# A third order table for a four-layer attention and mixture kernel: new marks for the same 5036 steps, all row fills in one run, and explicit waits where buffers are reused

## The chip, the cores and the metric

One Trainium2 chip, one core. The metric is the device time of one launch in microseconds, the median of the runs. A profile of one more execution gives the span from the first to the last instruction.

## The reference, cut to what matters

Eight batches of 256 tokens with 256 features pass four layers. Each layer is an attention with 16 heads of 16 features against a context of the same size, followed by a feed-forward part, and the feed-forward parts differ.

```
layer 0: x += attention(layernorm(x), ctx), causal;  x += layernorm(x) @ sign(W)
layer 1: x += attention(...), causal;                x += two shared experts + the best 2 of 16 experts
layer 2: x += attention(...), masked, q/k/v normed;  x += quantised gated product, 1024 wide, ternary weights
layer 3: x += attention without projections;         x += three blocks, each norm, gelu, two 256x256 products
```

The 16 experts of layer 1 are sparse: each token's row is copied to a place that depends on its expert, the rows are worked in 31 tiles of 128 rows for each half of the batches, and the results are copied back and added with their weights.

## The kernel before, in words

The kernel keeps the whole of `x` in SBUF. Its work is cut into 5036 **steps**, and a step is one method of a `Part` class. Every engine has its own `Part` with its own methods, so that a step is one engine's piece of work: `score` and `maxima` are TensorE's, `exp` and `projected` ScalarE's, `reduce` and `normalise` VectorE's, `k_low`, `scatter` and `fetch` GpSimd's, and `k_stack`, `fill`, `tile_load` and the other transfers SyncE's.

The steps stand in 378 **lanes**. A lane is a generator that gives its steps in a fixed order (the lane `exponents` gives all 512 `exp` steps, the lane `tile` those of one tile). The tuple `AT` holds for each lane one number, here called a **mark**, for each of its steps. `program` sorts all marks of all lanes and calls the steps in that order. Each engine's instruction stream is thus what is left of the sorted list when only its own steps are kept, and an engine never takes a step before the one ahead of it. The marks come from a planner that isn't part of the file. On the chip they mean nothing but order, with one exception: `claim` chooses the PSUM bank of a new tile by comparing marks with `DRAIN`, 0.6 after the mark of the step that empties a bank.

What must not happen before something else is said by semaphores. Where a buffer is reused and the code has no wait, the order of the table together with other waits keeps the two apart.

The order of attention is `ORDER`: 32 items (layer, batch), layers 0 and 1 mixed in the first half and 2 and 3 in the second. For each item:

- `k_hi`/`q_hi` (ScalarE, line 1931 to 1948), `k_rest`/`q_rest` (VectorE), `k_low`/`q_low` (GpSimd, 2658 and 2660) split keys and queries in three bf16 parts.
- `k_stack` and `q_stack` (SyncE, 2890) copy the parts to the stacked operands, six transfers of 128 KB each.
- 16 x `maxima` (TensorE, 1580) and `reduce` (VectorE, 2247, 2255 or 2259) find row maxima, and `turn_max` (1669) and `rows` (ScalarE, 2027) turn them.
- 16 x `score` (1598 with 1601 or 1604) and `exp` (ScalarE, 2010) follow, and then `values` (1688), `copy_output`, `output`, `normalise`, and the projection `project_in`, `projected`, `project_out`, `project_add`.

Beside attention run the fills (12 transfers from `wo` that give the two row buffers in HBM defined contents, line 2942), the raw weights of layer 2 (`raw_load`, 2983), 32 `scatter` and 32 `fetch` steps (GpSimd's indirect transfers, 2803 and 2816), and the tiles: `gather` loads an expert's weights (384 KB), `tile_load` a tile's rows (2960), `tile_turn`, `tile_up` and `tile_down` are its products, and `tile_store` writes it back. At the very end the last batch's three blocks run in two halves of 128 tokens (`half_in`, `half_turn`, `half_out` and so on, lines 1869 and 1874), and between exponentials and gelus ScalarE loads another function table.

`wait_score` on GpSimd, ahead of every `scatter` and `fetch`, waits for the last `score` whose mark lies before that of the step.

Of the kernel before, what the change touches and what calls it, by code (L numbers as in the profile page):

```python
# [12 lines left out]
P = 128  # L13
# [85 lines left out]
class Signal:  # L99
# [8 lines left out]

    def at(self, key):

        return self.sem, self.unit * (self.known.get(key, 0) + 1)
# [3 lines left out]
AT = (  # L115
# [1096 lines left out]
def build(nc, known, x_d, ctx_t_d, ctx_d, mask_d, mask_t_d, w_d, wo_d, vec_d, col_d, gate_d,  # L1212
          expert_d, wq_gate_d, wq_up_d, wq_down_d, w3_d, scale3_d, la_d, lb_d, out_d):
    made = {}
    with ExitStack() as ctx:
# [206 lines left out]
        def tile_of(key):  # L1422
            return ps[:, bank_of[key], :]
# [1695 lines left out]
```

## Time and profile before

| what | value |
|---|---|
| runs | 1161.19, 1162.01 and 1164.85 us; median 1162.01 |
| profiled execution | span 1166.1 us, 26103 instructions; no other time is given for it |
| busy | TensorE 1050.5, VectorE 903.8, ScalarE 804.5, GpSimd 564.1 us |
| TensorE's granted clock | 0.970 of full over the span |
| DMA | 140.03 MB, mean 120 GB/s |

The span is the time of one execution with the profiler on. A busy time is that of an engine's instructions; matmuls overlap, so that the busy time of TensorE is longer than the least time between its issues.

### The profile page before, as it was taken

The numbers are of one execution on the slowest core, as the hardware profiler recorded it, in microseconds if no ns is written. First come the engines' busy times: TensorE is split into PE (matmuls) and PEld (weight loads), VectorE is DVE, ScalarE is ACT, GpSimd is POOL, SyncE is SP. The second block draws the span as 40 slices with busy tenths as digits, with TensorE's granted clock in tenths as the row PEclk, the third lists the DMA queues.
The fourth block names the chain that finished last, engine by engine and source line by source line (L and its number), as shares of the span: only waits on it lengthen the run. The fifth ranks groups of instructions, "written<-read, shape, count | busy, mean of one in ns | idle before, by whom it ended". The sixth has DMA issues, their size and how long they took to land.

```text
span 1166.1 us, 26103 instructions
## 1 busy us (share of the span) xinstructions
PE 1050.5 (90%) x8259; PEld 782.0 (67%) x8298; DVE 903.8 (78%) x3323; ACT 804.5 (69%) x1484; POOL 564.1 (48%) x1161
## 2 busy tenths in 40 slices
PE   7989999999999989898888898788898989989986
PEld 6667877777887866676666765556665665656664
DVE  3879887877564688898885588999997889887643
ACT  5757666566674555566565667656989899998962
POOL 7232364655122365577830125766455454545443
PEclk9999999999999998999999999979999999999997
DMA  7985322325667643412258864232132222222000
GB/s 239 312 284 143 92 74 56 91 74 173 203 181 210 200 127 82 136 47 84 81 185 262 249 184 147 84 92 76 39 100 73 73 55 56 83 64 55 1 19 19
DMA packets 102327, 140.03 MB, mean 120 GB/s; under 512 B 12336, under 2 KB 79792, under 8 KB 102192
## 3 DMA queue, kind: packets, MB, share of 16 engines
q1 hardware_dynamic: 98688, 129.57, 38.0%
q0 software_dynamic: 3072, 8.39, 2.3%
q8 instruction: 69, 1.13, 0.4%
q14 instruction: 66, 0.54, 0.1%
q10 hardware_dynamic: 432, 0.39, 0.1%
HBM read 65.43 MB, written 22.54 MB: 75 GB/s over the span
## 4 chain that ended last, share of the span: by engine, by line
PE 40%; DVE 18%; ACT 15%; DMA 8%; issue 7%; SPq 5%; POOL 5%; another core or an unknown queue 1%; DVEq 0%; POOLq 0%; ACTq 0%
PE ps L1559 9%; PE ps L1688 4%; ACT probs L2010 4%; PE ps L1580 4%; PE ps L1598 4%; SPq L2890 3%; PE ps L1781 3%; PE ps L1552 3%; PE ps L1566 2%; ACT q_st L2027 2%; DVE ps L2247 2%; DMA w<-in_expert 2%; PE ps L1601 2%; DVE ps L2255 2%; PE ps L1748 1%
## 5 line engine op out<-in xcount | busy, mean ns | idle before, releaser
L2010 ACT ACTIVATE probs<-ps 128x384 f32<-128x384 f32 (+1 forms) x512 | 260.2, 545 | 91.4 <-PE ps L1601 46.4
L1580 PE MATMUL ps<-k_st,q_st 96*128 96x256 bf16 (+1 forms) x1024 | 172.4, 266 | 26.8 <-DVE neg_max L2247 10.3
L1598 PE MATMUL ps<-q_st,k_st 104*128 104x256 bf16 (+1 forms) x1024 | 178.0, 263 | 16.8 <-ACT probs L2010 12.3
L2027 ACT ACTIVATE q_st<-ps 8x1024 bf16<-8x1024 f32 x128 | 129.9, 1016 | 24.4 <-PE ps L1669 21.8
L1580 PEld LDWEIGHTS ps<-k_st,q_st 96*128 96x128 bf16 x1024 | 86.8, 100 | 79.1 <-DVE neg_max L2247 19.1
L2247 DVE CUSTOM_DVE_ANT_0 ps<-ps,diag_s 128x128 f32<-128x128 f32 (+1 forms) x384 | 123.3, 358 | 20.9 <-PE ps L1580 18.7
L1598 PEld LDWEIGHTS ps<-q_st,k_st 104*128 104x128 bf16 x1024 | 90.7, 99 | 61.7 <-issue 19.5
L1688 PE MATMUL ps<-probs,v 128*32 128x256 f32 (+1 forms) x2048 | 126.0, 365 | 2.0 <-ACT probs L2010 1.9
L2576 POOL TENSOR_SCALAR var_eps<-mv 128x2 f32<-128x2 f32 (+1 forms) x115 | 27.8, 242 | 185.2 <-DVE mv L2139 180.1
L2255 DVE CUSTOM_DVE_ANT_0 ps<-ps,mask_s 128x256 f32<-128x256 f32 x256 | 101.4, 452 | 6.2 <-PE ps L1580 5.8
L2658 POOL CAST parts<-qf 128x512 bf16<-128x512 f32 x64 | 40.5, 633 | 100.3 <-DVE qf L2166 44.7
L1688 PEld LDWEIGHTS ps<-probs,v 128*32 128x32 f32 x2048 | 55.0, 110 | 49.9 <-issue 25.8
L2259 DVE TENSOR_REDUCE neg_max<-ps 128x2 f32<-128x512 f32 x128 | 82.5, 680 | 5.4 <-PE ps L1580 2.9
L2581 POOL TENSOR_TENSOR rstd<-var_eps,neg_half 128x2 f32<-128x2 f32 (+1 forms) x115 | 84.4, 734 | 0.6
L2660 POOL TENSOR_TENSOR parts<-qf,parts 128x512 bf16<-128x512 f32 x64 | 75.0, 1173 | 5.2
L1559 PE MATMUL ps<-w,xn_t 128*128 128x256 f32 x296 | 74.1, 394 | 1.8 <-ACT xn_t L1906 1.2
L1959 ACT ACTIVATE xn<-x,shift,rstd 128x256 f32<-128x256 f32 x112 | 64.0, 633 | 16.2 <-POOL shift L2586 12.1
L1781 PE MATMUL ps<-ring,w 128*128 128x128 f32 x496 | 67.1, 281 | 6.5 <-DMA w<-in_expert 4.0
L2247 DVE DVE_READ_ACCUMULATOR2_ANT neg_max<- 128x1 f32 x512 | 72.5, 142 | 0.0
L1601 PE MATMUL ps<-diag_t,ident_b 128*128 128x256 bf16 x256 | 71.0, 278 | 0.0
L1781 PEld LDWEIGHTS ps<-ring,w 128*128 128x128 f32 x496 | 61.6, 193 | 12.1 <-issue 7.6
L1559 PEld LDWEIGHTS ps<-w,xn_t 128*128 128x128 f32 x296 | 54.7, 195 | 13.5 <-issue 6.8
(275 smaller groups left out, 2548.9 us busy)
## 6 DMA issues: line engine op xcount, KB each, us to landing
k_st<-parts SPq DMA_DIRECT2D x192, 128.0 KB
q_st<-parts SPq DMA_DIRECT2D x189, 128.0 KB, 2.8
w<-in_expert SPq DMA_DIRECT2D x62, 384.0 KB, 4.2
x_rows<-wo SPq DMA_DIRECT2D x10, 768.0 KB, 10.9
ctx_t<-in_ctx_t SPq DMA_DIRECT2D x16, 256.0 KB, 3.0
ring<-x_rows SPq DMA_DIRECT2D x31, 128.0 KB, 3.3
y_rows<-ring SPq DMA_DIRECT2D x31, 128.0 KB, 3.7
xn_t<-x_rows SPq DMA_DIRECT2D x31, 128.0 KB, 4.0
```

The costliest lines, as they stand in the source:

```text
L1559: last = mm(t[:, a * D:(a + 1) * D], act_t[:, kt, a * P:(a + 1) * P], weight[:, kt, :], start=kt == 0, stop=kt == KT - 1)
L1580: last = mm(t[:, c0:c0 + n], head(q_st, r, h, KROWS, j * P, P), head(k_st, r, h, KROWS, 0, n), start=j == 0 or not by_pe, stop=not by_pe, ...
L1598: last = mm(t[:, j * S:j * S + n], head(k_st, r, h, KALL, j * P, P), head(q_st, r, h, KALL, skip, n), start=j == 0 or L == 3, stop=L == 3, ...
L1601: last = mm(t.rearrange("p (j t) -> p j t", j=SJ)[:, :, 0:P], ident_b[:, :], diag_t[:, L, :, :], start=False, stop=True, skip_group_check= ...
L1688: last = mm(t[h4 * DPAD:(h4 + 1) * DPAD, skip:S], v[:, r, j, hg * HPG + h4, :], probs[:, (hg % 2) * HPG + h4, j * S:(j + 1) * S - skip], s ...
L1781: last = mm(t[:, n * P:(n + 1) * P], expert[:, i % RING, c0:c0 + INNER_E], x_tile_t[:, i % 2, kt * P:(kt + 1) * P], start=kt == 0, stop=kt ...
L2010: nc.scalar.activation(probs[:, (hg % 2) * HPG + h4, 0:width], tile_of(key)[:, 0:width], ACT.Exp, scale=SCALE).then_inc(*tile_drained(key))
L2027: nc.scalar.activation(out, tile_of(key)[KROWS:KALL, 0:S].unsqueeze(1).to_broadcast([2 * HPG, HPG, S]), ACT.Copy).then_inc(*tile_drained(key))
L2247: last = V.tensor_tensor_reduce(some, some, diag_s[:, n0:n0 + j * step + 1:step, :], -1.0, -NEG, ALU.add, ALU.min, neg_max[:, hg, h4, j:j ...
L2255: last = V.tensor_tensor_reduce(some, some, mask_s[:, b % 2, j, :], -1.0, -NEG, ALU.add, ALU.min, neg_max[:, hg, h4, j:j + 1])
L2259: V.tensor_reduce(neg_max[:, hg, h4, :], tile_of(key).rearrange("p (j t) -> p j t", j=SJ), AX.X, ALU.max, negate=True).then_inc(*tile_drai ...
L2581: G.tensor_tensor(rstd[:, kind, tiles], var_eps[:, kind, tiles], neg_half[:, 0:SJ if a is None else 1], ALU.pow).then_inc(*ln_rstd.step((p ...
```

## The change

- **The table.** `AT` is replaced. It has the same 378 lanes and the same 5036 marks, now in hundredths instead of tenths, and `program` divides by 100. The order of every engine changes: of TensorE's 1950 steps, 50 keep their place in the stream, of SyncE's 327, 31 do. `ORDER` stays, and `DRAIN` stays.
- **Waits added.** `projected` waits for the `project_out` before it (buffer `o_t`), `quantised_copy` for the hidden products of the batch before (`xq_t`), `down_copy` for the `down` two tiles before (`hid_t`), and `normalise` for the `normalise` of the item before. `load` of a context waits for all four readers of the buffer and not for one, `ctx_load(0)` for all items and not for the last, and the first tile loads of the second group for two batches and not for one.
- **A buffer.** `sum_inv` gets two halves.
- **Waits removed.** `wait_score` is gone, and with it a wait ahead of each `scatter` and `fetch`.
- `drain` returns the same semaphore and the same step as the expression that it replaces.

```diff
@@ the lane of the fills
-    (307, 313, 319, 336, 342, 348, 516, 543, 549, 555, 561, 567),
+    (3301, 3345, 3384, 3423, 3462, 3501, 3540, 3579, 3618, 3657, 3696, 3735),
@@ program
-        clock[0] = t / 10
+        clock[0] = t / 100
@@ ScalarE
                 def projected(L, b):
+                    n = SLOT[L, b] - 1
+                    while n >= 0 and ORDER[n][0] == 3:
+                        n -= 1
+                    if n >= 0:
+                        wait_filled(act, ("wo", *ORDER[n]))
                     drain(("op", L, b), o_t[:, :, :])
                 def quantised_copy(b):
+                    if b:
+                        for T in range((b - 1) * SJ, b * SJ):
+                            for c in range(2):
+                                wait_filled(act, ("hu", T, c))
                     wait_filled(act, ("xq", b))
                 def down_copy(T):
+                    if T >= SJ:
+                        wait_filled(act, ("hd", T - SJ))
@@ VectorE, normalise
+                    if SLOT[L, b]:
+                        wait_drained(dve, ("ot", *ORDER[SLOT[L, b] - 1], pair))
+                    inv = sum_inv[:, pair, :, :]
-                    V.reciprocal(sum_inv[:, :, :], t[:, :, :, DH]).then_inc(*inverted.step((L, b, pair)))
+                    V.reciprocal(inv, t[:, :, :, DH]).then_inc(*inverted.step((L, b, pair)))
@@ GpSimd, scatter and fetch
-                    wait_score()
@@ SyncE
             def load_batch(L, b):
-                if L == 0 and b >= 4:
-                    wait_filled(sp, ("v", 1, b - 4))
+                read = b - 4 if L == 0 else b + 4
+                if L == 0 and b >= 4 or L == 2 and b < 4:
+                    for what in ("k", "v"):
+                        for layer in range(2):
+                            wait_filled(sp, (what, layer, read))
                 def ctx_load(b):
                     if b == 0:
-                        sp.wait_ge(*x_bias.at((1, B - 1)))
-                        wait_drained(sp, ("v", 1, B - 1))
+                        for item in FIRST:
+                            sp.wait_ge(*x_bias.at(item))
+                        wait_all_drained(sp, [("v", *item) for item in FIRST])
                 def tile_load(i):
                     if GT <= i < GT + RING:
-                        wait_filled(sp, ("logit", LAST))
-                        wait_filled(sp, ("ed", LAST))
+                        for b in (B - 2, LAST):
+                            wait_filled(sp, ("logit", b))
+                            wait_filled(sp, ("ed", b))
```

The marks of some steps in both tables, each divided by its own unit (10 or 100):

| step | mark before | mark after |
|---|---|---|
| first `maxima` of item (0, 2) | 56.4 | 90.7 |
| first `exp` of item (0, 0) | 29.5 | 30.3 |
| first `exp` of item (0, 2) | 67.0 | 97.3 |
| first `exp` of item (1, 0) | 93.2 | 114.7 |
| first `exp` of item (1, 4) | 318.4 | 307.1 |
| first `exp` of item (1, 7) | 470.1 | 430.5 |
| first `exp` of item (2, 0) | 499.2 | 568.8 |
| first `exp` of item (3, 0) | 683.0 | 698.5 |
| first `exp` of item (2, 5) | 793.1 | 808.2 |
| last `exp` | 1057.1 | 1078.4 |
| last `half_out` | 1105.8 | 1115.5 |
| last step of all, `half_store(1)` | 1107.5 | 1117.1 |
| tile loads and stores, first half of the batches | 269.3 to 390.7 | 362.1 to 500.3 |
| tile loads and stores, second half | 563.1 to 661.5 | 510.3 to 653.5 |
| `scatter` steps | 151.1 to 557.7 | 243.2 to 505.1 |
| `fetch` steps | 396.1 to 710.3 | 506.4 to 702.2 |
| the six `raw_load` | 62.9 to 100.4 | 38.4 to 150.5 |

The least distance from the mark of a step to the mark of the next step on its engine, over all steps of a kind, is what the planner lets a step of this kind cost:

| steps | before | after |
|---|---|---|
| `maxima`, layers 0 and 1 / 2 and 3 | 0.10 / 0.20 | 0.17 / 0.23 |
| `score`, layers 0 and 1 | 0.20 | 0.27 |
| `values`, layers 0 and 1 | 0.70 | 0.93 |
| products of 8 passes, as `v_out` | 1.80 | 1.75 |
| `exp`, layers 0 and 1 / 2 and 3 | 0.30 / 0.40 | 0.39 / 0.48 |
| `exp` followed by a gelu | 1.90 | 1.78 |
| `scatter` | 1.00 | 1.36 |
| later of `k_stack` and `q_stack` to the first `maxima` (two least) | 5.0, 5.7 | 6.1, 6.8 |
| `tile_load` to its `tile_turn` | 2.4 | 5.3 |
| all of TensorE's steps, count times least distance, summed | 891 | 980 |

In the order of `exp` and gelu steps on ScalarE, 33 changes between the two stand before and 37 after.

## Rows read from the trace of the kernel before

**Rows 1.** The page: engines' busy time and the span in 40 slices.
```profile
span 1166.1 us, 26103 instructions
...
PE 1050.5 (90%) x8259; PEld 782.0 (67%) x8298; DVE 903.8 (78%) x3323; ACT 804.5 (69%) x1484; POOL 564.1 (48%) x1161
...
DMA  7985322325667643412258864232132222222000
```

**Rows 2.** Busy time by stretch: us, PE, PEld, DVE, ACT, POOL, clock, DMA.
```profile
0.00:50.00 50.00, 41.31 (x288) 31.50 (x289) 28.21 (x135) 30.41 (x48) 26.52 (x66) 0.93 0.89 279
50.00:100.00 50.00, 44.52 (x397) 35.45 (x395) 40.98 (x178) 33.18 (x64) 14.74 (x29) 0.97 0.75 238
100.00:200.00 100.00, 96.28 (x875) 76.67 (x875) 84.14 (x403) 69.63 (x136) 45.19 (x96) 1.00 0.33 91
...
300.00:400.00 100.00, 94.06 (x759) 79.28 (x758) 57.50 (x249) 60.44 (x146) 23.60 (x49) 0.98 0.71 201
...
600.00:700.00 100.00, 89.44 (x667) 70.22 (x676) 66.97 (x242) 60.77 (x145) 15.41 (x24) 1.00 0.77 226
...
800.00:1112.00 312.00, 284.98 (x2261) 193.21 (x2276) 262.14 (x723) 282.71 (x448) 161.59 (x325) 0.99 0.23 63
```

**Rows 3.** Line 2010 (`exp`) from the first of an item on: count, first and last start.
```profile
L2010 ACT ACTIVATE probs<-ps x512: 466/562/685, 32.4 to 1112.7; 128x384 f32<-128x384 f32 x86, 128x512 f32<-128x512 f32 x85
...
L2010 ACT ACTIVATE probs<-ps x480: 466/586/685, 71.5 to 1112.7; 128x512 f32<-128x512 f32 x85, 128x384 f32<-128x384 f32 x75
...
L2010 ACT ACTIVATE probs<-ps x464: 466/588/685, 102.9 to 1112.7; 128x512 f32<-128x512 f32 x85, 128x384 f32<-128x384 f32 x70
...
L2010 ACT ACTIVATE probs<-ps x336: 468/596/685, 332.5 to 1112.7; 128x512 f32<-128x512 f32 x128, 128x384 f32<-128x384 f32 x40
...
L2010 ACT ACTIVATE probs<-ps x272: 475/597/685, 499.5 to 1112.7; 128x512 f32<-128x512 f32 x128, 128x384 f32<-128x384 f32 x8
...
L2010 ACT ACTIVATE probs<-ps x144: 575/597/647, 848.4 to 1112.7; 128x512 f32<-128x512 f32 x144
```

**Rows 4.** The chain that ended last, a full stretch of TensorE: start, us, what.
```profile
86.54 0.79 PE ps L1688 x16
87.33 0.27 PE ps L1598 x2
87.60 0.11 PE ps L1601
87.71 0.17 PE ps L1598 x2
87.88 0.11 PE ps L1601
87.99 1.73 PE ps L1559 x8
89.72 0.17 PE ps L1580 x2
```

**Rows 5.** DMA issues by line: count, size, median us from issue to landing.
```profile
q_st<-parts SPq DMA_DIRECT2D x189, 128.0 KB, 2.8
...
x_rows<-wo SPq DMA_DIRECT2D x10, 768.0 KB, 10.9
...
ring<-x_rows SPq DMA_DIRECT2D x31, 128.0 KB, 3.3
...
xn_t<-x_rows SPq DMA_DIRECT2D x31, 128.0 KB, 4.0
```

**Rows 6.** The first six fills (line 2942), issued 33.6 to 38.4.
```profile
L2942 SPq DMA_DIRECT2D x_rows<-wo x6: 442/520/957, 33.6 to 38.4; - x6
...
DMA to landing us min/median/max: 7.7/10.9/13.4
```

**Rows 7.** The chain that ended last, around one `q_stack` (item (1, 7)).
```profile
470.88 0.55 SPq L2890
...
474.09 4.92 DMA q_st<-parts
479.01 0.14 issue
479.14 0.49 PE ps L1580 x4
```

**Rows 8.** GpSimd in order of time: three scatters back to back.
```profile
276.04 0.98 POOL L2803 DMA_INDIRECT x_rows<-xn,dest  x1 [0.30 <-issue]
277.32 0.96 POOL L2803 DMA_INDIRECT x_rows<-xn,dest  x1 [0.30 <-issue]
278.58 0.96 POOL L2803 DMA_INDIRECT x_rows<-xn,dest  x1 [0.30 <-issue]
```

**Rows 9.** Who GpSimd waited for ahead of indirect transfers: us, times, longest.
```profile
POOL ring L2816 <- PE ps L1601: 5.1, 3, 1.8
POOL xn_t L2816 <- PE ps L1598: 4.2, 3, 2.2
...
POOL x_rows L2803 <- PE ps L1601: 4.0, 4, 1.3
...
POOL x_rows L2803 <- PE ps L1604: 2.2, 2, 1.4
```

**Rows 10.** ScalarE in order of time, around one load of a function table.
```profile
941.96 1.10 ACT L2010 ACTIVATE probs<-ps 128x512 f32<-128x512 f32 x2
942.91 1.11 ACT L1959 ACTIVATE w<-w,shift,rstd 128x256 f32<-128x256 f32 x2
944.04 1.28 ACT L2122 ACT_TABLE_LOAD   x1
945.34 1.02 ACT L2122 ACTIVATE ring<-ps,col 128x256 f32<-128x256 f32 x2
```

**Rows 11.** Table loads by line: count, busy us, mean ns, idle before.
```profile
L2122 ACT ACT_TABLE_LOAD x17 | 21.8, 1283 | 0.3
L2010 ACT ACT_TABLE_LOAD x16 | 20.5, 1283 | 0.3
```

**Rows 12.** Waits without work at line 1433: ns min/median/max.
```profile
L1433 ACTq EVENT_SEMAPHORE  x407: 17/17/2004, 17.2 to 1134.6; - x136
L1433 DVEq EVENT_SEMAPHORE  x250: 21/21/746, 17.9 to 1163.4; - x125
L1433 SPq EVENT_SEMAPHORE  x68: 17/17/28, 294.1 to 697.8; - x68
```

More of the change, by code:

```diff
@@ L107, in step, with drain @@
         return self.sem, self.unit
+    def drain(self, key):
+        return self.sem, self.unit
     def at(self, key):
@@ L1257, in build @@
         own = sb("own", [P, HPG], BF16)
-        sum_inv = sb("sum_inv", [P, SJ, 2 * HPG])
+        sum_inv = sb("sum_inv", [P, 2, SJ, 2 * HPG])
         bn = sb("bn", [P, 3, NT, 6])
@@ L1429, in tile_drained @@
             new_drain_at[key] = clock[0] + DRAIN
-            return drained[bank_of[key]].sem, 1
+            return drained[bank_of[key]].drain(key)
         def wait_filled(eng, key):
@@ L2280, in normalise @@
                     wait_filled(dve, key)
+                    if SLOT[L, b]:
+                        wait_drained(dve, ("ot", *ORDER[SLOT[L, b] - 1], pair))
+                    inv = sum_inv[:, pair, :, :]
                     t = tile_of(key).rearrange("p (a h e) -> p a h e", a=SJ, e=DPAD)
-                    V.reciprocal(sum_inv[:, :, :], t[:, :, :, DH]).then_inc(*inverted.step((L, b, pair)))
+                    V.reciprocal(inv, t[:, :, :, DH]).then_inc(*inverted.step((L, b, pair)))
                     dve.wait_ge(*inverted.at((L, b, pair)))
                     out = o_tok[:, r, :, pair * 2 * HPG * DH:(pair + 1) * 2 * HPG * DH].rearrange("p a (h d) -> p a h d", d=DH)
-                    V.tensor_tensor(out, t[:, :, :, 0:DH], sum_inv[:, :, :].unsqueeze(3).to_broadcast([P, SJ, 2 * HPG, DH]), ALU.mult).then_inc(
+                    V.tensor_tensor(out, t[:, :, :, 0:DH], inv.unsqueeze(3).to_broadcast([P, SJ, 2 * HPG, DH]), ALU.mult).then_inc(
                         *tile_drained(key))
@@ L2587, in power @@
                     *ln_shift.step((p, b)))
-            def wait_score():
-                n = sum(10 * clock[0] > t for t in AT[0])
-                if n:
-                    L, b = ORDER[(n - 1) // H]
-                    wait_filled(pool, ("s", L, b, *divmod((n - 1) % H, HPG)))
             class Part(Idle):
@@ L2814, in fetch @@
                             pool.wait_ge(*y_out[i % RING].at(i))
-                    wait_score()
                     G.indirect_dma_start(y_in(b, n), None, y_rows[g],
@@ L2856, in load_batch @@
             def load_batch(L, b):
-                if L == 0 and b >= 4:
-                    wait_filled(sp, ("v", 1, b - 4))
+                read = b - 4 if L == 0 else b + 4
[3 more added lines that the diff above has]
+                            wait_filled(sp, (what, layer, read))
                 if L == 2:
-                    if b < 4:
-                        wait_filled(sp, ("v", 1, b + 4))
-                    else:
+                    if b >= 4:
+                        for what in ("k", "v"):
+                            wait_filled(sp, (what, 2, b - 4))
                         sp.wait_ge(*part_rest.at(("k", 3, b - 4)))
```

1087 rows, old and new, of the table AT are left out of this document.

## The prediction

> **What bounds the kernel now.** I read the page first: TensorE is busy for 90% of the span, VectorE for 78%, ScalarE for 69%, GpSimd for 48% [rows 1]. Then the stretches [rows 2]. From 100 to 200 us TensorE is busy for 96 of 100 us with a third of the DMA time used. Ahead of 100 us, DMA is 89% and 75% busy and TensorE has its first holes. From 300 to 400 and from 600 to 700, where the tiles run, DMA is 71% and 77% busy and TensorE falls to 94 and 89. From 800 on ScalarE is the fullest beside TensorE (283 against 285 of 312 us). So no single engine is the bound: TensorE nearly is one in the first half, and everywhere the frozen order of each engine turns every late input into idle time that nothing else may fill.
>
> The useful view is therefore a comparison of marks with the trace. If the planner's picture were exact, the trace would stand at a constant distance from the marks. The starts of line 2010 [rows 3] minus the marks of the same `exp` steps give how far the chip had fallen behind the table:
>
> - 32.4 - 29.5 = 2.9 us at the first;
> - 71.5 - 67.0 = 4.5 at item (0, 2);
> - 102.9 - 93.2 = 9.7 at (1, 0), after the fills;
> - 332.5 - 318.4 = 14.1 at (1, 4);
> - 499.5 - 470.1 = 29.4 at (1, 7), after the first group's tiles and fetches;
> - 848.4 - 793.1 = 55.3 at (2, 5), after the second group's;
> - 1112.7 - 1057.1 = 55.6 at the last.
>
> The span ends 58.6 after the last mark (1166.1 against 1107.5). The lag has a pattern: 4.4 us in the 225 marks from 93.2 to 318.4 and 0.3 us in the 264 marks from 793.1 to 1057.1, but 46 us in the stretches with fills, tiles, scatters and fetches. It grew where data moved, not where the engines were fullest.
>
> **The change part by part.** The marks are no time of the chip, and I use them only with the lag that rows give them.
>
> *The table's end.* The last mark goes from 1107.5 to 1117.1, so with equal lag the kernel would be 9.6 us slower. All of the gain must come from a smaller lag.
>
> *Why the lag arose, and what the new marks allow for.* I compare the least distances in the two tables with rows.
> - `q_stack` to `maxima`: before at least 5.0. The stack of (1, 7) took 479.14 - 470.88 = 8.3 us [rows 7], where the old marks leave 6.1. After: at least 6.1, then 6.8.
> - Scatters: before 1.00, after 1.36. The rows give 1.27 from start to start [rows 8].
> - Tile rows: before 2.4 from load to turn, after 5.3. The landing takes 3.3 or 4.0 [rows 5], with some 0.4 to start the products.
> - `exp`: before 0.30 and 0.40. Two of the wider ones take 1.10 with their overlap, about 0.5 each [rows 10]; after 0.39 and 0.48.
> - TensorE: `values` takes 0.79 and a product of 8 passes 1.73 [rows 4]; before 0.70 and 1.80, after 0.93 and 1.75. A causal `score` takes 0.28 (0.17 and 0.11), before 0.20, after 0.27.
>
> Every old price that is under its row has been raised to it or above it. So I take the lag of the loaded stretches, which came from these prices, as gone, and keep the rate of the quiet ones: 4.4 + 0.3 = 4.7 us in 489 marks, 1%, over 1117 marks 10.7. Bounds: 0 (the new prices lie above the rows, and the quiet rate was earned with prices under them) and 52.7 (55.6 - 2.9, all of it comes back). I take 10, near the low end, because the quiet stretches show that the rest of the picture holds.
>
> *Start and end.* The first `exp` was 2.9 late, and the end 3.0 later than the last `exp`'s lag (58.6 - 55.6). Both stay: +5.9. The tail itself is well drawn: from the last `exp` to the end of the span 53.4 us against 50.4 marks. In the new table it is 38.7 marks long, because ten of TensorE's turns and products for batches 5 and 6 are left for it and not fifteen.
>
> *The fills.* The table puts all 12 in one run of 4.4, where before six stood at 31 and six at 52 to 57. They are not spread out. The first six landed between 33.6 + 7.7 = 41.3 at the earliest and 38.4 + 13.4 = 51.8 [rows 6]: four of 768 KB, one of 128 KB and 512 KB of masks in 10.5 us, some 365 GB/s. The 12 are 7936 KB, so 22 us from about 39, done near 61. The stacks of (0, 2), marked 46.2 and 50.0, stand behind them in SyncE's queue and can land by some 67. The new table lets the first `maxima` of (0, 2) begin at 90.7 only. So here the chip may lead its table, by up to 20 us. VectorE and TensorE must have other work ready for that, and a lead is lost where another input binds. I take 8, bounds 0 and 20.
>
> *Table loads on ScalarE.* 33 changes between `exp` and gelu become 37. A load takes 1.28 and nothing stands between it and the gelu (944.04 + 1.28, then 945.34) [rows 10], as for all 33 [rows 11]: 4 x 1.30 = 5.2 us more on ScalarE. Both tables have this price in their marks (after: 1.78 - 0.48 = 1.30), so it is in the 1117.1 and adds nothing again. The Trainium skill (ScalarE: Activation LUTs, What ACT_TABLE_LOAD costs) adds a drain of about 1.38 us to each load. By it, the four more would cost 10.6 and not 5.2, and the forecast would be 5 us later; the row shows no such gap, and I go by the row.
>
> *The waits.* Added ones cost 17 to 21 ns each in the sequencer where they are met [rows 12]; some 65 on ScalarE and 62 on VectorE, together 2.4 us that lie in work already priced above its rows. Whether they are met, the marks say. `projected` follows the `project_out` that it waits for by 4.1 at least, (2, 3) after (2, 2), and its product takes 1.7; the others by 9 or more. If it is late, the exponentials behind it on ScalarE wait too, and TensorE's `score` steps after them. `quantised_copy` has 9.3, `down_copy` 24.6, `normalise` 11.9. On SyncE the first tile load of group 2 (510.3) now waits for `shared_down(6)` at 505.2, 3.4 us of room; late, it holds the gathers and stacks behind it. The contexts' and `ctx_load(0)`'s waits name readers whose steps lie before the one that was waited for already. I take 0, bounds 0 and 3.
>
> *`wait_score` gone, `sum_inv` doubled.* GpSimd stood 15.5 us in 12 such waits [rows 9]. It is busy for 48% of the span [rows 1], and what stood behind the scatters had marks that assume no wait. I take 0; the gain could be a few microseconds in `merge`, the loss a scatter that holds `k_low` where it had stood later: 1.27 us each at most. The second half of `sum_inv` removes no wait that the code has.
>
> **The sum.** 1117.1 + 5.9 + 10 - 8 = 1125.0 as a span. The median of the runs was 4.1 us under the profiled span (1166.1 against 1162.0). That leaves 1121, 3.5% less than before.
>
> **The rivals.**
>
> *Ahead of the table.* The new prices of TensorE lie over the rows by 5% or so, the tile landings by 1.3 us, and the front by 20. Between marks 100 and 500 the table has TensorE at 392 (steps times new prices); 5% of that is 20. Then 1117.1 + 5.9 - 20 - 8 - 4.1 = 1091. For it: TensorE in the rows is faster than its prices. Against it: the quiet stretches, with TensorE under 96%, still lagged by 1%.
>
> *Half of the lag stays.* Prices are right, but a frozen order turns variation into idle time. With 26 of the 52.7: 1117.1 + 5.9 + 26 - 4.1 = 1145. For it: ScalarE from 800 on and TensorE are packed tighter than before. Against it: the end of the old table kept a constant lag with ScalarE at 91%.
>
> *TensorE's pace.* The new table wants 392 of 400 from TensorE from 100 to 500. The steps which the trace shows in 100 to 200 are worth 96 at the new prices, those in 300 to 400, beside the tiles, 90 [rows 2]. If TensorE does no more than 90 per 100 us, 392 takes 435 us: +35. With the 10: 1117.1 + 5.9 + 35 + 10 - 4.1 = 1164, no change. For it: from 362 to 500 the tiles run there again. Against it: the old marks asked no more in that stretch, so it shows no limit.
>
> *The lag comes back (slower).* One mechanism: transfers that land later than marked, while the engines' orders leave no other work, between the fills and the last lora load. Before it cost 52.7; the same again gives 1117.1 + 5.9 + 52.7 - 4.1 = 1172. It decides from 42 on. For it: the same bytes, in SyncE's one queue. Against it: tiles are spread over 281 marks (362.1 to 500.3 and 510.3 to 653.5) and not 220, and the landings are priced above the rows.
>
> **How the numbers follow.** The forecast, 1105 to 1138, has 0.46. Half of the lag 0.21, ahead of the table 0.18, TensorE's pace 0.05, the lag back 0.10. The likeliest gives 1121. The range of 8 in 10 is 1090 to 1158: it leaves out half of the case ahead and all of the last two, some 0.2. A change within 0.3% is about what a measurement of this kernel can't tell from none (1158.5 to 1165.5): 0.05. Faster by more: 0.85. Slower by more: 0.10.
>
> **What the profile after would show.** First `exp` of (0, 2) between 75 and 97 and of (1, 0) between 100 and 117, if the fills cost what I say. Lag of line 2010 at (2, 0), mark 568.8, between -10 and +12; at the last `exp`, mark 1078.4, between -5 and +15 against 55.6. 37 table loads ahead of `exp` and gelu instructions. The last `exp` 41 to 43 us ahead of the end and not 53. TensorE 95% busy or more from 100 to 500. Wrong would be: a lag over 20 at (1, 7), mark 430.5, which would speak for TensorE's pace; a lag that jumps between (2, 0) and (2, 5), which would speak for late landings; a long wait of SyncE ahead of the first tile load of group 2; or a wait at `projected`.

## The result, and the profile after

The changed kernel takes 1175.61 us (median of 4 runs, 1170.89 to 1177.48), the kernel before 1161.6 in the same comparison (4 runs, 1156.94 to 1164.85). The ratio is 1.0114, 95% interval 1.0073 to 1.0154: slower by 1.1%, where 3.5% faster was forecast. The profiled execution took 1177.48, its span is 1175.7. The page answers to [rows 1], with the clock's line added:

```profile
span 1175.7 us, 26177 instructions
...
PE 1044.2 (89%) x8260; PEld 782.2 (67%) x8298; DVE 894.3 (76%) x3323; ACT 811.5 (69%) x1488; POOL 568.4 (48%) x1161
...
PEclk9878999999999999998899998899999999999999
DMA  8943242423223776735877454322312112322000
```

Work is as much as before and the span is longer, so the loss is idle time. The stretches (columns as in [rows 2]: TensorE, its weight loads, VectorE, ScalarE, GpSimd, clock, DMA share, GB/s) say where:

```profile
50.00:100.00 50.00, 32.57 (x261) 23.55 (x254) 18.98 (x95) 19.33 (x37) 9.22 (x15) 0.83 0.49 161
100.00:200.00 100.00, 91.02 (x784) 68.70 (x784) 80.53 (x377) 65.05 (x124) 30.65 (x55) 0.95 0.35 100
300.00:400.00 100.00, 95.49 (x873) 77.03 (x872) 80.32 (x402) 66.82 (x132) 59.48 (x139) 1.00 0.38 110
600.00:700.00 100.00, 94.34 (x771) 71.96 (x782) 85.30 (x340) 75.70 (x151) 29.63 (x48) 1.00 0.59 176
800.00:1133.00 333.00, 305.02 (x2417) 209.96 (x2437) 294.11 (x785) 301.82 (x475) 165.81 (x328) 0.99 0.21 59
```

From 300 to 400 and from 600 to 700 TensorE is fuller than before, as the table wanted. From 50 to 100 it is busy for 32.6 us at a granted clock of 0.83; before it was 44.5 us at 0.97. The lag is read as in the prediction, from the starts of the `exp` line (2042 now) on from the first of an item, here (0, 1), (0, 2), (1, 7), (2, 0) and (3, 0):

```profile
L2042 ACT ACTIVATE probs<-ps x496: 466/578/692, 75.2 to 1133.2; 128x512 f32<-128x512 f32 x86, 128x384 f32<-128x384 f32 x80
L2042 ACT ACTIVATE probs<-ps x480: 466/581/692, 118.7 to 1133.2; 128x512 f32<-128x512 f32 x85, 128x384 f32<-128x384 f32 x75
L2042 ACT ACTIVATE probs<-ps x272: 467/597/692, 457.1 to 1133.2; 128x512 f32<-128x512 f32 x128, 128x384 f32<-128x384 f32 x8
L2042 ACT ACTIVATE probs<-ps x256: 572/597/692, 605.8 to 1133.2; 128x512 f32<-128x512 f32 x128
L2042 ACT ACTIVATE probs<-ps x192: 572/597/692, 742.6 to 1133.2; 128x512 f32<-128x512 f32 x192
```

Less their marks (57.7, 97.3, 430.5, 568.8, 698.5) this is 17.5, 21.4, 26.6, 37.0 and 44.1, and 1133.2 - 1078.4 = 54.8 at the last. Two thirds of the lag arise in two places, at the front (1.8 to 21.4) and between (1, 7) and (3, 0) (26.6 to 44.1).

The front is one wait. The chain that ended last shows the stack of k of item (0, 2):

```profile
50.83 0.94 SPq L2930
...
55.00 4.42 SPq L2930
59.47 11.53 DMA k_st<-parts
71.07 0.85 ACT parts L1969 x2
...
72.34 0.47 DVE qf L2207
```

and the three engines in order of time show who stood behind it (in brackets the idle time ahead, and what ended it):

```profile
71.07 0.84 ACT L1969 ACTIVATE parts<-ps,col 128x256 bf16<-128x256 f32 x2 [12.93 <-DMA k_st<-parts]
...
71.94 0.88 DVE L2207 SCALAR_TENSOR_TENSOR qf<-ps,col,parts 128x256 f32<-128x256 f32 x2 [12.20 <-ACT parts L1969]
...
74.12 0.50 PE L1612 MATMUL ps<-k_st,q_st 96*128 96x128 bf16 x2 [13.43 <-DVE neg_max L2290]
```

Line 1969 is `k_hi(1, 0)`. It overwrites `parts`, and so waits (in `split_hi`) until the last of the six blocks of the stack before has been read out of it. Its mark is 53.35, 7.1 after the stack's 46.21; the chip needed 20.2 (50.83 to 71.07), as 12 fills stood ahead in SyncE's queue: one of the stack's own six issues took 4.42, and its last block 11.5 to land. Nothing that reads (0, 2) was late. The next writer of the buffer was.

### The profile page after: what moved, and what is told of

It is laid out like the page before. It is cut to its first block, busy times and chain, and to the rows that moved or that the text cites. A ratio compares the mean times of both kernels' runs of the same rounds, so it can differ in the third digit from the quotient of the medians.

```text
span 1175.7 us, 26177 instructions
## 1 busy us (share of the span) xinstructions
PE 1044.2 (89%) x8260; PEld 782.2 (67%) x8298; DVE 894.3 (76%) x3323; ACT 811.5 (69%) x1488; POOL 568.4 (48%) x1161
## 4 chain that ended last, share of the span: by engine, by line
PE 38%; DVE 28%; ACT 15%; issue 8%; POOL 5%; DMA 4%; SPq 2%; another core or an unknown queue 0%; DVEq 0%; POOLq 0%; ACTq 0%
PE ps L1591 8%; DVE ps L2290 4%; ACT probs L2042 4%; PE ps L1720 4%; PE ps L1630 3%; PE ps L1612 3%; PE ps L1584 3%; DVE ps L2298 3%; PE ps L1813 3%; DVE bn L2179 3%; ACT q_st L2059 2%; PE ps L1598 2%; DVE neg_max L2302 2%; DMA k_st<-parts 2%; SPq L2930 1%
## 5 line engine op out<-in xcount | busy, mean ns | idle before, releaser
L1630 PE MATMUL ps<-q_st,k_st 104*128 104x256 bf16 (+1 forms) x1024 | 176.9, 262 | 16.4 <-ACT probs L2042 10.3
L2290 DVE CUSTOM_DVE_ANT_0 ps<-ps,diag_s 128x128 f32<-128x128 f32 (+1 forms) x384 | 123.0, 358 | 17.8 <-PE ps L1612 17.3
L1630 PEld LDWEIGHTS ps<-q_st,k_st 104*128 104x128 bf16 x1024 | 90.0, 99 | 59.3 <-ACT probs L2042 18.2
L1813 PEld LDWEIGHTS ps<-ring,w 128*128 128x128 f32 x496 | 64.7, 198 | 3.5 <-ACT ring L2094 0.8
L1591 PE MATMUL ps<-w,ctx_t 128*128 128x256 f32 x256 | 65.2, 400 | 0.3 <-ACT q_st L2059 0.3
```

What stands on the lines that cost most here:

```text
L1591: last = mm(t[:, a * D:(a + 1) * D], act_t[:, kt, a * P:(a + 1) * P], weight[:, kt, :], start=kt == 0, stop=kt == KT - 1)
L1630: last = mm(t[:, j * S:j * S + n], head(k_st, r, h, KALL, j * P, P), head(q_st, r, h, KALL, skip, n), start=j == 0 or L == 3, stop=L == 3, ...
L1813: last = mm(t[:, n * P:(n + 1) * P], expert[:, i % RING, c0:c0 + INNER_E], x_tile_t[:, i % 2, kt * P:(kt + 1) * P], start=kt == 0, stop=kt ...
L2290: last = V.tensor_tensor_reduce(some, some, diag_s[:, n0:n0 + j * step + 1:step, :], -1.0, -NEG, ALU.add, ALU.min, neg_max[:, hg, h4, j:j ...
```

## The experiments

Each batch ran beside its own runs of the kernel before, on one chip a batch; ratios are to those, and a lag is read as above. Ratios compare all runs, but a lag is that of the one execution that was profiled, so differences of a few microseconds in lag between batches prove little.

**Batch 1.** e1 takes the fills of the new table out of the stack's way. e2 gives the old table the new one's single run of fills. e3 is the old table with all code changes. e4 is the changed kernel with `wait_score` back.

```diff
 e1, the changed kernel
-    (3301, 3345, 3384, 3423, 3462, 3501, 3540, 3579, 3618, 3657, 3696, 3735),
+    (5200, 5500, 5800, 6100, 6400, 6700, 8800, 9100, 9400, 9700, 10000, 10300),
 e2, the kernel before
-    (307, 313, 319, 336, 342, 348, 516, 543, 549, 555, 561, 567),
+    (307, 313, 319, 336, 342, 348, 354, 360, 366, 372, 378, 384),
```

> The changed kernel with one lane of the table altered: the 12 fills get marks 52 to 67 and 88 to 103, behind the stacks of item (0, 2), and not 33.0 to 37.4. Theory A (SyncE's one queue: k_stack(0, 2) is issued behind 8 MB of fills, lands at 71, and ScalarE stands at k_hi(1, 0), which may not overwrite the parts before that): the lag at the first exp of (0, 1) falls from 17.5 to about 3, and the kernel gains 15 to 20 us against the change, some 1157. Rival B (the lag comes from DMA traffic or from a table too full for TensorE, and would appear later anyway): the gain is under 6 us, 1170 or more.

> The kernel before with its six later fills (marks 51.6 to 56.7) moved up behind the first six, 35.4 to 38.4, so that all 12 go ahead of the stacks of (0, 2). Theory A: those stacks land about 12 us later, ScalarE stands at k_hi(1, 0) by as much less the room that was there, and the kernel is 5 to 12 us slower than before. Rival B: the same bytes moved by 15 us change nothing, within 3 us of before.

> The table of before, all of the rest of the change: the added waits, the two halves of sum_inv, no wait ahead of scatters and fetches. Theory A: the waits are met when they come and cost 17 to 21 ns each, within 3 us of before. Rival C (the explicit waits or the free scatters cost the loss): 10 us or more slower than before.

> The changed kernel with the wait ahead of each scatter and fetch put back. Theory A: within 3 us of the change, 1173 to 1178, since GpSimd has room. Rival D (scatters that go as soon as they may disturb what the marks assume): 4 us or more faster than the change.

| | ratio | 95% interval | lag at (0, 1) | at (2, 0) | at the last |
|---|---|---|---|---|---|
| before | 1 | | 3.6 | 28.1 | 55.6 |
| after | 1.0114 | 1.0073 to 1.0154 | 17.5 | 37.0 | 54.8 |
| e1 | 0.9982 | 0.9956 to 1.0008 | 3.8 | 21.8 | 39.8 |
| e2 | 1.0017 | 0.9996 to 1.0038 | 6.0 | 34.5 | 60.3 |
| e3 | 1.0042 | 1.0021 to 1.0063 | 3.1 | 31.3 | 54.9 |
| e4 | 1.0108 | 1.0085 to 1.0131 | 17.3 | 37.5 | 51.6 |

The `exp` line of e1 on from (0, 1):

```profile
L2042 ACT ACTIVATE probs<-ps x496: 465/578/698, 61.5 to 1118.2; 128x512 f32<-128x512 f32 x86, 128x384 f32<-128x384 f32 x80
```

All but 1.3 of the 15.0 us by which e1 ends nearer to its table are there at the first `exp` of (0, 1), and they stay to the end. In e2 the same run of fills costs the old table 12.8 at (0, 2) (lag 17.3 for 4.5), but 4.7 at the last, in a profile that is the slowest of e2's runs. By the medians it costs 1.8 us, which can't be told from nothing; 5 to 12 were expected. Most of it is thus hidden later; in which waits, no run shows. e3 is 4.3 us slower by the medians, between its two expectations. `wait_score` is nothing in the new table (e4).

**Batch 2.** e5 leaves the fills in one run and moves the wait: the four steps of k of (1, 0) stand after its stack's landing. If it is as good as e1, late stacks cost time only through the order on ScalarE, and the traffic costs none by itself. e6 and e7 part e3: waits alone, free scatters alone. e8 moves `lora_load(0)` behind the stack of (3, 0) in e1.

```diff
 e5, the changed kernel: k_out, k_hi, k_rest, k_low of (1, 0)
-    (4599, 5335, 5482, 5579, 7658),
+    (7092, 7180, 7270, 7360, 7658),
 e7, the kernel before (twice)
-                    wait_score()
```

> The changed kernel, fills in one run as it has them, but the keys of item (1, 0) split later: k_out, k_hi, k_rest and k_low from marks 46.0, 53.4, 54.8 and 55.8 to 70.9, 71.8, 72.7 and 73.6, behind 11 exponentials of item (0, 1). Theory A (the loss is what stands behind a waiting k_hi on ScalarE, not the traffic): the lag at the first exp of (0, 1) falls from 17.5 to 5 or less, and most of the 16 us that moving the fills gave come back here too, 1157 to 1165. Rival B (late stacks hold TensorE by themselves): (0, 2) is late anyway and the gain is under 6 us, 1169 or more.

> The table of before with the added waits and the halves of sum_inv, and the wait ahead of scatters and fetches kept. The code alone cost 4.9 us (0.42%). If the added waits cost it: 3 to 5 us slower than before, 1165 to 1167. If not: within 2 us.

> The kernel before without the wait ahead of scatters and fetches, nothing else. If this part of the code cost the 4.9 us: 3 to 5 us slower than before. If not: within 2 us. In the changed kernel, putting the wait back gave nothing, which speaks for the second.

> The fills behind the stacks as in e1, and the first low-rank load, 768 KB of vectors with it, moved from ahead of the query stack of item (3, 0) to behind it (mark 69.9 less 600 becomes 676.0, its three later steps 684.5). Theory A: the stack lands 3 to 5 us earlier, the lag grows by 3 instead of 7.5 from (2, 3) to (3, 0), and the kernel gains 2 to 5 us on e1, 1154 to 1157. Rival B: the time is lost a little later, same as e1 within 2 us.

e5: 0.9989 (0.9962 to 1.0016), lag 3.6 at (0, 1), 15.8 at (2, 0), 27.1 at the last. So the loss needs both, a stack made late by the fills (e1 takes that away) and the order behind `k_hi` (e5 does): with the fills where the change put them, the front's loss is gone. That e5 ends 12.7 nearer to its table than e1 at the same ratio is no gain of the kernel: its profile is the fastest of its runs, and its chip ran the kernel before in 1155.6 and not 1162.1. e6: 1.0058 (1.0032 to 1.0084). e7: 0.9942 (0.9915 to 0.9968), faster than both kernels. e8: 0.9997 (0.9975 to 1.002), no gain over e1. TensorE's wait of 3.9 for the stack of (3, 0) is gone, but at the same step it waits 2.6 for VectorE, and from (2, 3) to (3, 0) the lag grows by 4.9 for 7.5. In e5, which leaves the load in its place, it grows by 1.6. So this load isn't shown to cost anything.

**What is left between (1, 7) and (3, 0).** In e1 the table itself leaves TensorE a hole of 7.5 ahead of `token_turn(k, 0)`: four scatters and four fetches stand in GpSimd's order ahead of the step (`token_power`) that makes the factors which ScalarE needs. ScalarE and TensorE of e1 in order of time:

```profile
515.96 1.97 PE L1591 MATMUL ps<-w,ctx_t 128*128 128x256 f32 x8
517.76 1.89 PE L1790 MATMUL ps<-vec,xn_t 128*128 128x256 f32 x8
...
526.25 1.09 ACT L1991 ACTIVATE w<-w,shift,rstd 128x256 f32<-128x256 f32 x2 [9.80 <-POOL shift L2632]
...
527.49 1.09 PE L1598 MATMUL ps<-ident,w 128*128 128x128 f32 x4 [7.83 <-ACT w L1991]
528.37 3.62 PE L1591 MATMUL ps<-w,ctx_t 128*128 128x256 f32 x8
```

The hole is planned for. What is not: the granted clock fell from 1.0 to 0.5 (2.4 to 1.2 GHz) in it and stayed there for 10.2 us, and the same product of 8 passes takes 3.62 after it for 1.97 ahead of it. So **batch 3** fills holes with matmuls whose result is overwritten (in `claim`, ahead of the tile's own), each run shorter than its hole:

```diff
-IDLE = {}
+IDLE = {("kt", 0): 32, ("xt", "l2a", 1): 14, ("qt", 1): 8, ("gd", 41): 10, ("m", 3, 0, 0, 0): 14}
```

e12 is e9 without the added waits. e10 and e11 part the waits in the old table.

> The kernel e5 (the changed kernel with the fills in one run and the hi part of k of (1,0) later) with throw-away matmuls (identity by a constant, 128x512 bf16, about 0.21 each) put on TensorE ahead of five tiles where it stands idle: 32 ahead of the turn of token k(0), 14 ahead of the turn for l2a(1), 8 ahead of the turn of token q(1), 10 ahead of the expert product 41, 14 ahead of the first maxima of (3,0). Each run is shorter than the hole it lies in (8.2, 4.0, 2.3, 3.2, 4.2 us), so no step has to start later. The results of these matmuls are overwritten. Theory C: half of the lag of 27 that e5 still ends with is the granted clock, which fell to 0.5 for 10.2, 6.8 and 3.4 us right after these holes and for 6.8 at 722; the planner has no such price. Then the granted clock stays at 1.0 in 510 to 600, the lag at the first exp of (2,0) is 7 to 9 in place of 15.8, and the ratio to the kernel before is 0.980 to 0.990 (e5: 0.9989). Rival D: the steps of that stretch are slower than planned for reasons of their own (GpSimd's scatters, the weight rings), and the low clock only shows that TensorE waited: then the lag at (2,0) stays at 14 to 16 and the ratio within 0.996 to 1.001.

> The kernel e9 with all added waits taken out again and sum_inv back at one half (the scatters stay free). If the added waits cost in the new table what lies between e7 and e3 in the old one (1.0%), the ratio is 0.008 to 0.012 below that of e9; if they cost nothing, the two agree within 0.003. With theory C right it is the fastest so far, 0.975 to 0.990.

> The order table of before; of the code changes the two calls of wait_score taken out (as in e7) and the added waits of ScalarE and VectorE with the second half of sum_inv, none of SyncE's. Theory: the waits of ScalarE and VectorE are on steps long done and cost nothing: ratio as e7, 0.991 to 0.997. Rival: they carry the 1.0% that lies between e7 (0.9942) and e3 (1.0042): ratio 0.999 to 1.006.

> The order table of before; wait_score taken out, and the added waits of SyncE alone (ahead of the batch loads, of the context load and of the rows of the first five tiles of a group), none of ScalarE's and VectorE's. Theory: SyncE's waits are on steps that are done by then and cost nothing: ratio as e7, 0.991 to 0.997. Rival: one of them holds SyncE's queue, and the loads and stacks queued behind it come later: ratio 0.999 to 1.006, with SyncE idle ahead of a load where e7 is not.

e9: 0.9971 (0.9953 to 0.9988), e12: 0.9954 (0.9933 to 0.9975). TensorE of e9 in order of time:

```profile
519.86 7.07 PE L1450 MATMUL ps<-diag_s,ident_b 128*128 128x512 bf16 x32
527.66 0.66 PE L1598 MATMUL ps<-ident,w 128*128 128x128 f32 x4 [0.73 <-ACT w L1991]
528.15 1.89 PE L1591 MATMUL ps<-w,ctx_t 128*128 128x256 f32 x8
```

The clock stays up and the product takes 1.89. From mark 513 to 557, ScalarE's lag rises by 4.1 in e1 and by 0.1 in e9. But Theory C had more: the ratio was to be 0.980 to 0.990 and is 0.9971, which lies in rival D's range and isn't told from e5's, and the lag at (2, 0) was to be 7 to 9 and is 20.5. Of the 4.7 by which that is above e5's 15.8, all is there at (1, 7), ahead of every filler (11.7 for 6.8; e9's profile is the slowest of its runs); from there to (2, 0) the two grow alike, by 8.8 and 9.0. Two of the five fillers lie in no hole in e9: TensorE runs from the last of them straight into the step behind (they take 4.0 and 3.2 us). And one wait is untouched: ScalarE's `token_hi(k, 2)` waits for the stack of `token k(1)`, the front's mechanism again, 4.3 us in the changed kernel and 4.9 in e9.

**Batch 4** therefore has e14 (e12 with the three good fillers), e13 (e14 with that step of ScalarE behind the five that stood behind it), e16 (the changed kernel, nothing undone, with four fillers, 52 matmuls of them in the front's hole) and e7 once more (e15).

```diff
 e13
-    (53108, 53497, 54300, 54460, 55134, 55766, 56042, 56269, 59252),
+    (53108, 53497, 54300, 54460, 55134, 56195, 56470, 56697, 59252),
 e16, the changed kernel
+IDLE = {("t", 0, 1, 0): 52, ("kt", 0): 32, ("xt", "l2a", 1): 14, ("qt", 1): 8}
```

> The kernel e12 (order table of after with fills in one run and k hi of (1,0) later, free scatters, no added waits) with throw-away matmuls ahead of three tiles alone: token k(0), l2a(1), token q(1). The fillers ahead of the expert product 41 (10, 2.1 us) and of the maxima of (3,0) (14, 3.0 us) are gone, as TensorE no longer stood idle there. Expected: 3 to 5 less lag at (3,0) than e12 and a ratio of 0.991 to 0.994 (e12: 0.9954). If those two had lain in real holes, the ratio is that of e12 or above.

> The kernel e14 with one step of ScalarE moved in the order table: the hi part of token k(2) goes from mark 557.66 to 561.95, behind the two steps apply k(3) and the four tile steps that stood behind it (its rest part on VectorE to 564.70, its low part on GpSimd to 566.97). Theory E: ScalarE waits there for the stack of token k(1) to land, with work of its own queued behind; then that wait shrinks below 1, the lag at the exp of (2,0) is 3 to 4 below that of e14, and the ratio 0.002 to 0.004 below that of e14. Rival: the stack lands no earlier and VectorE and the stacks behind take up the delay: the same lag at (2,0) within 1 and a ratio within 0.001.

> The changed kernel itself, nothing undone, with throw-away matmuls (128x512 bf16) put into four of TensorE's holes: 52 ahead of the turn of the maxima of (0,1), group 0, inside the 13.4 that TensorE stands idle at 61 to 74, and 32, 14 and 8 ahead of token k(0), l2a(1) and token q(1). ScalarE's wait for the stack of k (0,2) stays as it is. Theory C: the half clock after a hole costs what it slows: the granted clock stays at 1.0 in 61 to 80 and 538 to 575, the lag at (0,1) stays at 17 to 18, that at (0,2) is 18 to 19.5 in place of 21.4, that at (2,0) 4 to 7 lower than 37.0, and the ratio is 1.004 to 1.007 (after: 1.0114). Rival: the lag is set by the waits alone: 37 at (2,0) within 1.5, ratio 1.009 to 1.013.

> The kernel e7 once more, on another chip: before with the two calls of wait_score taken out and nothing else. If the gain of e7 is one of the kernel, the ratio is 0.990 to 0.997 again, and the added waits cost 0.7 to 1.0% (e10, e11). If it was the chip of that batch, the ratio is 0.999 to 1.004, and neither the free scatters nor the waits do anything that can be told from nothing.

e14: 0.9942 (0.9915 to 0.9968), at the edge of what was expected and not told apart from e12; its lag at (3, 0) is 17.2 for 22.6, but 3.3 of those 5.4 are there at (1, 7), ahead of both fillers taken out. e13: **0.9918** (0.989 to 0.9945), the lowest ratio of the study. The `exp` line on from (2, 0), first e14, then e13:

```profile
L2042 ACT ACTIVATE probs<-ps x256: 571/597/692, 581.9 to 1103.7; 128x512 f32<-128x512 f32 x128
```

```profile
L2042 ACT ACTIVATE probs<-ps x256: 572/597/700, 580.3 to 1103.0; 128x512 f32<-128x512 f32 x128
```

The idle time of 2.09 ahead of that step in e14 is gone in e13, but the lag at (2, 0) falls by 1.6 and not by 3 to 4, and the intervals of the ratios overlap: in place and sign as expected, too small to be told apart. What the steps behind (1, 7) gained is clearer from (1, 7) to (2, 0): the lag grows by 9.0 in e5, 5.5 in e14 and 3.0 in e13.

e16: 1.0054 (1.0026 to 1.0082) against 1.0114 of the changed kernel (1.0108 in e4), in Theory C's range and out of its rival's, though the intervals of e16 and of the changed kernel just overlap. Three stretches of 20 us, first the changed kernel's, then e16's (PE, PEld, DVE, ACT, POOL, clock, DMA):

```profile
60.00:80.00 20.00, 6.46 (x48) 3.80 (x46) 6.56 (x33) 4.78 (x9) 3.10 (x6) 0.58 0.60 161
...
540.00:560.00 20.00, 16.24 (x86) 13.67 (x87) 9.68 (x29) 9.24 (x23) 15.89 (x26) 0.80 0.53 153
560.00:580.00 20.00, 15.22 (x92) 13.78 (x91) 10.55 (x33) 12.12 (x30) 14.85 (x26) 0.83 0.91 256
```

```profile
60.00:80.00 20.00, 17.76 (x118) 9.69 (x118) 8.72 (x48) 7.11 (x13) 3.10 (x6) 1.00 0.60 161
...
540.00:560.00 20.00, 17.57 (x115) 15.19 (x115) 14.37 (x41) 11.62 (x31) 17.42 (x27) 1.00 0.72 200
560.00:580.00 20.00, 17.65 (x111) 13.59 (x111) 11.12 (x35) 13.75 (x32) 17.63 (x29) 1.00 0.90 271
```

Its `exp` line from (2, 0) on:

```profile
L2042 ACT ACTIVATE probs<-ps x256: 570/597/691, 593.8 to 1115.8; 128x512 f32<-128x512 f32 x128
```

The wait at the front is there (ScalarE 12.0 us, lag 16.1 at (0, 1)), yet e16 is 593.8 - 568.8 = 25.0 behind at (2, 0), where the changed kernel is 37.0, and 37.4 at the last for 54.8. By the medians the gain is 0.0060 x 1160 = 7 us, by the two profiles 17; e16's profile is the fastest of its runs and that of the changed kernel the slowest of its own, so I go by 7. The trace has some 6 of it behind fillers: 2.4 from (0, 1) to (0, 2) and 3.6 between marks 513 and 551. Of the 12.0 at (2, 0), where 4 to 7 were expected, another 1.7 arise from (0, 6) to (1, 4), where no filler stands and the changed kernel has a pause of the kind told next. The changed kernel wasn't run on e16's chip, so up to a few microseconds of the 7 may be the chip's.

**The waits in the old table.** e10: 1.0043 (1.0012 to 1.0074); e11: 1.0034 (1.0005 to 1.0062); e15: 0.9927 (0.9903 to 0.9952), so e7's gain came again on a second chip. Both expectations "cost nothing" fell: each half of the waits stands 1.0 to 1.1% above the free scatters alone, and the two together (e3) no further, so it is not the sum of the waits' prices. But e7 and e15 ran on other chips than e3, e10 and e11, and the chips differ. ScalarE of e15, of e11 and of e6 at the same step (the copy of `o_raw`), the first two with the sixteen matmuls that it reads:

```profile
409.01 0.86 PE L1688 MATMUL ps<-probs,v 128*32 128x256 f32 x16
...
410.00 0.60 ACT L2020 ACTIVATE o_raw<-ps 128x512 f32<-128x512 f32 x1 [0.33 <-PE ps L1688]
```

```profile
409.76 0.86 PE L1691 MATMUL ps<-probs,v 128*32 128x256 f32 x16
...
413.21 0.60 ACT L2023 ACTIVATE o_raw<-ps 128x512 f32<-128x512 f32 x1 [2.18 <-remote]
413.85 0.30 DVE L2250 CUSTOM_DVE_ANT_0 ps<-ps,diag_s 128x128 f32<-128x128 f32 x1 [2.18 <-remote]
...
417.48 0.38 ACT L2053 ACTIVATE xn_t<-ps 128x256 f32<-128x256 f32 x1 [3.67 <-remote]
```

```profile
410.65 0.60 ACT L2023 ACTIVATE o_raw<-ps 128x512 f32<-128x512 f32 x1 [0.41 <-PE ps L1691]
412.62 0.38 ACT L2058 ACTIVATE xn_t<-ps 128x256 f32<-128x256 f32 x1 [1.37 <-PE ps L1751]
```

In e11, which adds no wait to either engine, ScalarE and VectorE stand still for 2 to 4 us with their input long done, and the profile knows no releaser (`remote`). On the chain such pauses sum to 13.1 us in e11, 13.3 in e3, 7.4 in e10 and 8.8 in the kernel before, and to nothing in e6, e7 and e15. They go with the batch and so with the chip, whatever the edit: all eight profiles of batches 1 and 3, and those of the two kernels compared, have such a pause of 1.5 to 3.9 us on ScalarE between 410 and 440, and the eight of batches 2 and 4 have none there. e6 has every wait and no pause. What they are stays open. They also aren't what the waits cost: e6 and e7 ran on one chip, neither has a pause on its chain, and e6 is 1.2% above e7. Nor can the waits and `wait_score`, which e6 keeps, be told apart by that pair. So on that chip the added waits cost the old table 0.6% over the kernel before (e6) and taking `wait_score` out gains 0.6% (e7); the way is open, and the free scatters alone were never run on a chip that has the pauses.

## Why the prediction was wrong, by its steps

**The sum.** 1117.1 + 5.9 + 10 - 8 = 1125 as a span; it was 1175.7. That is 1117.1 + 58.6. Start and end cost 1.8 + 3.8 = 5.6 (forecast 5.9); the rest is lag, 53.0, where I had 10 - 8 = 2. The offset from span to median was 0.1 and not 4.1. The rival "the lag comes back", 1172 with a chance of 0.10, was the outcome, in its mechanism too: transfers that land later than marked while the engines' orders leave no other work.

**The step that failed first: the fills, -8.** I had the stacks of (0, 2) land by 67 (that of k landed at 71.0) and asked only who reads them: `maxima` at 90.7, so a lead of up to 20. The buffer that they are read from has a next writer, `k_hi(1, 0)` at 53.4, ahead of it in ScalarE's order of everything else. e1 and e5 show that this costs 13 to 15 us. The term was +14 and not -8, and its bounds, 0 and 20 of gain, did not hold it, as I excluded a loss without following `split_hi`'s wait.

**The step that failed second: "it grew where data moved, so the new prices remove it", 10.** From (0, 2) to the last the lag still grew by 33.4. The prices were indeed right: TensorE is 98, 95 and 96% busy in 200 to 500, and in e5 the lag grows by 1.6 from (0, 2) to (1, 7). What grew it, as far as the runs show, has no price in the table: the halved clock after a hole (up to 7 us by e16's median, a third of it ahead of (0, 2)), and the same head-of-line wait at `token_hi(k, 2)` (idle 4.3). Another 6.5 came from (2, 3) to (3, 0), around a late stack; e8 turned none of it into time, and its cause is open. And 9 us from (2, 4) to the last in the changed kernel (45.8 to 54.8), e5 (18.2 to 27.1) and e16 (28.5 to 37.4) alike, where ScalarE and TensorE are both over 90% busy; I had 3.3 for it by the quiet rate of 1%. Its cause I haven't tried.

**Waits and `wait_score`, 0.** Right for the new table within what can be measured: e4 0.9994 of the changed kernel, e12 0.9983 of e9, both inside the intervals. In the old table, on one chip, they move 1.2% (e6 against e7), by a way that I had no price for and that is still open.

**Table's end, table loads, tail: right.** The last `exp` is 42.5 ahead of the end (41 to 43), and the loads are 37:

```profile
L2165 ACT ACT_TABLE_LOAD x19 | 24.4, 1283 | 1.2 <-PE ps L1598 0.8
L2042 ACT ACT_TABLE_LOAD x18 | 23.1, 1283 | 1.8 <-PE ps L1630 1.6
```

They take 1283 ns as before, ScalarE stands idle for 3.0 us ahead of all 37 together, and the gelu or `exp` behind starts within 0.02 us of the load's end. The Trainium skill (ScalarE: Activation LUTs, What ACT_TABLE_LOAD costs) adds a drain of about 1.38 us to each load. The trace shows none of that length behind any of the 37.

**A reading that misled.** "A lag over 20 at (1, 7) would speak for TensorE's pace": it was 26.6, and e1 and e5 have 11.1 and 6.8 there with the same work. Up to there the pace was not the limit. The other signs: the lag jumped by 10.3 from (2, 0) to (2, 5), 6.5 of it ahead of (3, 0); the first tile load of group 2 went at 541.4, right behind the gathers ahead of it, with no long wait; TensorE was busy for 95% from 100 to 500, but for 91% in the first hundred.

## What to carry to other kernels

For a transfer, ask not only when its reader needs it but which instruction overwrites its source, and what stands behind that instruction on its engine: one wait of 12.9 us on ScalarE held three engines, and moving four marks gave 1.2% back. A planner whose prices come from rows still lacks what happens after its own holes; throw-away matmuls in holes that the order can't avoid gave up to 0.6%, and cost their own length where there was no hole. Where profiles of two chips differ, an effect is safe only if both kernels ran on one of them. And the old table with two lines of waits removed (0.9935, mean of two chips) can't be told from the repaired new one (0.9918 to 0.9942).

## What the runs showed of the hardware

- The granted clock went to 0.5 in the long holes of TensorE shown here (13.4 us at 61 to 74, 7.8 at 520 to 527 in e1) and stayed there for 17 and 10 us. It also fell without one: at 232.6 in the kernel before, where no idle stretch in the 10 us ahead is over 0.61. It is at 0.5 for 83 us in all in the changed kernel, 72 before, 32 in e16. Eight passes then take 3.62 us for 1.89.
- An issue of a stack's 128 KB takes 0.60 in the median of all 381 in the changed kernel. The six behind 12 fills took 0.94, 1.03, 1.43, 0.61, 4.42 and 1.58; the last block landed 11.5 us after its issue.
- Pauses of 2 to 4 us of ScalarE and VectorE without a releaser, at the same steps on the chips of batches 1 and 3 (e3; e10 and e11), and none there on the chips of batches 2 and 4. Within a batch, edits elsewhere in the program change their number and length (e2 against e3).
